# One core, a four-layer transformer stack: the shared expert's chunks put into loops, and the rows of empty routing slots written to DRAM during attention

## The chip, the core and the metric

The kernel runs on one core of a Trainium2 chip. Its engines are TensorE (PE, matrix products; PEld is its weight load), VectorE (DVE), ScalarE (ACT), GpSimd (POOL) and SyncE (SP). Each has its own instruction stream, and they meet through semaphores. SP issues DMAs, and POOL issues the indirect ones, whose rows go to places given by an index. The metric is the time of one launch in microseconds (us) on the device, and less is better.

## What is computed

Eight sublayers on 4 x 1024 tokens of 128 features, each `x = x + f(layernorm(x))`. The change touches the first four: attention with 16 heads of 8 (layers 0 and 1), a gated mixture of experts in which every token goes to its two best of eight experts and to a shared one (layer 0), and a mixture in which every token goes to one of eight experts (layer 1).

```python
# layer 0, feed-forward
topk_logits, topk_idx = jax.lax.top_k(xf @ gate_w.T, 2)
topk_w = jax.nn.softmax(topk_logits)
for e in range(8):
    y = silu(xf @ wg[e].T) * (xf @ wu[e].T) @ w_down[e].T
    out = out + comb[:, e:e + 1] * y          # comb: topk_w, scattered to the experts
shared = silu(xf @ sg_gate.T) * (xf @ sg_up.T) @ sg_down.T
return shared + out
# layer 1, feed-forward: out = W2[e] applied to relu(W1[e] x + b1[e]) + b2[e] of the one expert e
```

## The kernel before

The activations stay in SBUF, transposed: `g.xT` and the normalised `g.xn` are 128 features by 4096 tokens, and a chunk is 512 tokens (`CH`), so there are eight chunks (`NCH`). The program is a row of stages (`Stage`). In a stage each engine has a block of its own, and a stage begins only when all engines are through with the one before, SP's waits among them: when a stage ends, SP clears its semaphores, and the next stage begins behind a barrier.

The stages that matter here, in order:

- `attention_stage` (L431). 32 pairs of heads and batches. In a pair PE makes the scores twice: once for the row maxima, which DVE reduces (L640), two pairs ahead, and once transposed, which ACT exponentiates (L625); PE then weighs the values (L564). POOL fetches the next queries and keys from DRAM (L478) and splits the maxima (L487). SP sends the maxima of the pair after next through DRAM into rows of the queries (`rows`, L511 and L514), which PE waits for before that pair, and stores the results (L523, L525). ACT's code is four pairs written out (m = 0) and a loop over the others, four pairs an iteration.
- `pick_stage` (L999), name f0r. Routing of layer 0: logits, the two best experts, and for each of the 8192 token copies the number of its slot. Slots stand in 39 blocks of 256 (`PICK_BLOCKS`), so that a block has one expert; 9984 slots in all, of which some stay empty. A slot's row is 132 floats (528 bytes): 128 features and a tail of four, with the row's place in the result and its weight. SP first writes all 9984 rows as zeros into `f0_sent` in DRAM (L1036), waits for that, and then writes their tails, each with a place of its own behind the results (L1039), and waits for those too (L1040). So rows of empty slots hold zeros, and a place that disturbs nothing.
- `pick_glu_stage` (L1150), name f0. POOL scatters the 64 tiles of 128 token rows to their slots (L1187), and SP, when all have landed, loads the slots back, six tiles of 128 at a time (L1203, `f_xs`). Meanwhile PE, ACT and DVE compute the shared expert, chunk by chunk: `shared_up` (L1218, L1219), SiLU (L1301), product (L1347), `shared_down` (L1226), addition to `g.xT` (L1340). PE's order is up(0), up(1), down(0), up(2), down(1) and so on, all written out. Then come the 39 blocks (L1235 and on), whose results POOL scatters to `f0_back` (L1193).
- `top1_stage` (L1431), name f1r, and `expert_stage` (L1614): the same for layer 1, with 5888 slots in 23 blocks. POOL clears a buffer `empty` of 46 rows a partition (L1465), DVE puts the places in (L1534), and SP writes it to `f1_sent` in one DMA (L1472) and waits. DVE and PE then look for each expert's threshold in 14 rounds (L1544 to L1560).

Of the kernel before, what the change touches and what calls it, by code (L numbers as in the profile page):

```python
# [14 lines left out]
F32 = mybir.dt.float32  # L15
# [48 lines left out]
class Weights:  # L64
# [16 lines left out]
    def load(self, sp):  # L81
        for tile, source in self.moves:
            sp.dma_start(tile, source, allow_slow_non_contiguous=True).then_inc(self.here, 16)

# [346 lines left out]
def attention_stage(nc, g, name, vsb, qstk, kstk, num, den, scale):  # L431
# [3 lines left out]
    with Stage(nc, name) as s:  # L435
# [24 lines left out]
        UNITS, CUTS = 32, 16  # L460

        with nc.Block() as block:
            @block.gpsimd
            def _(pool):
# [148 lines left out]
            def _(act):  # L613
# [128 lines left out]
def attention(nc, g, name, qkv, out, rope, scale, factor, ahead):  # L742
# [5 lines left out]
    with nc.sbuf_tensor(f"{name}_v", [P, NT, P], F32) as vsb:  # L748
        qkv_stage(nc, g, name + "_qkv", qkv, vsb, qstk, kstk, rope, ahead)
        attention_stage(nc, g, name + "_att", vsb, qstk, kstk, num, den, scale)  # L750
# [235 lines left out]
class Picked:  # L986
# [3 lines left out]
    def __init__(self, nc, ctx):  # L990
# [4 lines left out]
        self.sent = nc.dram_tensor("f0_sent", [PICK_SLOTS, PICK_WIDE], F32, kind="Internal").ap()  # L995
        self.back = nc.dram_tensor("f0_back", [2 * TOK + PICK_SLOTS, P], F32, kind="Internal").ap()


def pick_stage(nc, g, name, w, picked):  # L999
# [4 lines left out]
    n_rows = PICK_SLOTS // P  # L1004
    with Stage(nc, name) as s:
# [5 lines left out]
        zero, tail = s.sb("zero", [P, PICK_WIDE]), s.sb("tail", [P, n_rows, 4])  # L1011
# [9 lines left out]
        zeroed, numbered, own_ready, cleared = (s.sem(x) for x in ("zeroed", "numbered", "own_ready", "cleared"))  # L1021
        by_tile = lambda ps: ps[:, :].rearrange("p (t e) -> p t e", e=e)
        with nc.Block() as block:
            @block.gpsimd
            def _(pool):
                pool.memset(zero[:, :], 0.0).then_inc(zeroed, 1)
                pool.wait_ge(w.here, w.all)
                found.pad(pool)
                pool.memset(tail[:, :, :], 0.0).then_inc(zeroed, 1)
# [31 lines left out]
            def _(dve):  # L1061
# [12 lines left out]
                dve.wait_ge(zeroed, 3)  # L1074
                dve.tensor_scalar(tail[:, :, 0], number[:, :], float(2 * TOK), None, ALU.add).then_inc(numbered, 1)
                link(dve.tensor_copy(rows[:, 0, :, P], number[:, 0:NT]))
                link(dve.tensor_copy(rows[:, 1, :, P], number[:, NT:2 * NT]))
# [72 lines left out]
def pick_glu_stage(nc, g, name, w, picked, ahead):  # L1150
# [6 lines left out]
    with Stage(nc, name) as s:  # L1157
# [24 lines left out]
        with nc.Block() as block:  # L1182
            @block.gpsimd
            def _(pool):
                rows = picked.rows[:, :].rearrange("p (t d) -> p t d", d=PICK_WIDE)
                for t in range(2 * NT):
# [26 lines left out]
            def _(pe):  # L1213
                def shared_up(c):
                    for t in range(2):
                        if c >= 1:
                            pe.wait_ge(s_h, 2 * (c - 1) + t + 1)
                        pe.matmul(za[:, t, :], shared[:, t, :], g.xn[:, cols(c)], start=True, stop=True)  # L1218
                        pe.matmul(zb[:, t, :], shared[:, 2 + t, :], g.xn[:, cols(c)], start=True, stop=True).then_inc(s_ready, 1)  # L1219

                def shared_down(c):
                    if c >= 2:
                        pe.wait_ge(s_added, c - 1)
# [1534 lines left out]
```

## Time and profile before

| | |
|---|---|
| time of the launch, median of 3 | 3518.85 us (3512.96 to 3518.86) |
| the profiled execution's own time | 3530.75 us |
| its span, first to last instruction | 3529.0 us |
| TensorE clock granted, mean | 0.886 of full speed |
| busy: PE, DVE, ACT, POOL | 77%, 71%, 52%, 25% |
| first attention / pick stage / shared expert / blocks of f0, begin at | 213 us (first evacuation) / 881 / 922 / 1025 |

Rows of the timeline give start, duration, engine, line, operation, tiles and, in brackets, how long the engine stood idle before and what it waited for. "PEq" and "SPq" are an engine's sequencer; a wait for "PEq L1023" is the barrier of the block in line 1023. "issue" and "remote" mean that the profile shows nothing on the core that ended the wait.

### The profile page before, as it was taken

How to read it: one execution, taken by the hardware profiler on the slowest of the kernel's cores; microseconds unless marked ns; L12 is line 12 of the kernel's file. 1: busy time of each engine (PE TensorE's matmuls, PEld its weight loads, DVE VectorE, ACT ScalarE, POOL GpSimd, SP SyncE). 2: the span in 40 equal slices, each digit the busy share in tenths (PEclk: the TensorE clock that was granted, in tenths of full speed). 3: DMA queues.
4: the chain of work that ended last, by engine and by line, in shares of the span. 5: the costliest groups of instructions: out<-in, count | busy, mean ns of one | idle time of the engine just before them, and what ended most of it. 6: DMA issues, size and time to landing. Idle time of an engine off the chain costs nothing. (4 is left out here: it accounts for less than half of the span.)

```text
span 3529.0 us, 43620 instructions
## 1 busy us (share of the span) xinstructions
PE 2701.9 (77%) x12690; PEld 967.9 (27%) x12690; DVE 2505.7 (71%) x2942; ACT 1823.1 (52%) x3161; POOL 882.6 (25%) x985
## 2 busy tenths in 40 slices
PE   6499999984469649999998424867777777996666
PEld 3022222221136412222222114622222232332222
DVE  4699999963236469999996271288999975446548
ACT  2188888881224128888888102355555531224233
POOL 3311111100446221111110006416777740000000
PEclk8599999996789759999999657987999998998878
DMA  4200101003522330100100312111000000001010
GB/s 120 91 24 23 28 23 28 23 15 89 90 70 67 106 117 24 28 24 24 27 23 15 102 35 74 48 51 38 6 12 12 7 0 1 0 0 59 6 42 24
DMA packets 161483, 140.96 MB, mean 40 GB/s; under 512 B 51941, under 2 KB 135781, under 8 KB 160984
## 3 DMA queue, kind: packets, MB, share of 16 engines
q1 hardware_dynamic: 142040, 98.68, 10.5%
q0 software_dynamic: 19328, 40.87, 3.8%
q8 instruction: 57, 0.93, 0.1%
q14 instruction: 58, 0.48, 0.0%
HBM read 73.85 MB, written 65.62 MB: 40 GB/s over the span
## 5 line engine op out<-in xcount | busy, mean ns | idle before, releaser
L640 DVE TENSOR_REDUCE a_att_mx<-a_att_s 128x2 f32<-128x1024 f32 x1024 | 1204.9, 1219 | 77.8 <-PE a_att_s L551 65.7
L625 ACT ACTIVATE a_att_pt<-a_att_st 128x512 f32<-128x512 f32 x2048 | 1064.5, 603 | 246.9 <-PE a_att_st L577 246.3
L577 PE MATMUL a_att_st<-a_att_qst,a_att_kst 50*128 50x512 bf16 x2048 | 620.7, 385 | 63.9 <-ACT a_att_pt L625 51.6
L551 PE MATMUL a_att_s<-a_att_kst,a_att_qst 50*128 50x512 bf16 x2048 | 524.8, 399 | 85.1 <-DMA a_att_kst<-a_kstk 52.2
L564 PE MATMUL a_att_av<-a_att_pt,a_att_vst 128*32 128x512 f32 x4096 | 547.2, 607 | 0.0
L577 PEld LDWEIGHTS a_att_st<-a_att_qst,a_att_kst 50*128 50x128 bf16 x2048 | 157.9, 94 | 727.1 <-ACT a_att_pt L625 668.7
L2191 POOL TENSOR_TENSOR g_xn<-m2s_hs,m2s_cb 128x1024 f32<-128x1024 f32 x128 | 300.8, 2355 | 119.0 <-DVE m2s_hs L2158 68.7
L2158 DVE TENSOR_TENSOR_SCAN m2s_hs<-m2s_da,m2s_bps 128x1024 f32<-128x1024 f32 x128 | 292.7, 2287 | 4.4
L487 POOL CAST a_att_mt_in<-a_att_nmax 128x16 bf16<-128x16 f32 x64 | 12.6, 196 | 1072.7 <-DVE a_att_nmax L648 1072.7
L2074 PE MATMUL m2s_yps<-g_xn,g_ident 128*128 128x512 f32 x512 | 242.8, 597 | 0.9
L2130 ACT COPY m2s_cb<-m2s_cps 128x1024 f32<-128x1024 f32 x128 | 129.5, 1012 | 184.1 <-POOL g_xn L2191 182.5
L551 PEld LDWEIGHTS a_att_s<-a_att_kst,a_att_qst 50*128 50x128 bf16 x2048 | 112.8, 94 | 240.1 <-DVE a_att_mx L640 170.6
L2153 DVE TENSOR_TENSOR m2s_bps<-m2s_dtx,m2s_bps 128x1024 f32<-128x1024 f32 x128 | 154.6, 1208 | 3.9 <-POOL m2s_dtx L2177 3.9
L2125 ACT ACTIVATE m2s_da<-m_dt,m2s_aneg 128x1024 f32<-128x1024 f32 x128 | 147.4, 1151 | 0.0
L2094 PE MATMUL m2s_bps<-m_bcs,m2s_sel 96*128 96x512 bf16 x256 | 79.2, 392 | 85.2 <-DVE m2s_hs L2158 82.5
L163 POOL MEMSET n_mean_w<- 128x128 f32 x8 | 1.6, 204 | 565.9 <-POOLq L917 232.6
L959 ACT ACTIVATE f_sg<-f_gp 128x512 f32<-128x512 f32 x72 | 43.0, 597 | 181.5 <-PE f_cp L948 181.5
L971 DVE TENSOR_TENSOR f_h<-f_sg,f_up 128x512 f32<-128x512 f32 x72 | 49.5, 688 | 121.8 <-ACT f_sg L959 121.8
L270 ACT ACT_TABLE_LOAD x9 | 11.5, 1283 | 226.6 <-PEq L696 108.1
L2074 PEld LDWEIGHTS m2s_yps<-g_xn,g_ident 128*128 128x128 f32 x512 | 97.0, 191 | 85.2 <-issue 63.9
L564 PEld LDWEIGHTS a_att_av<-a_att_pt,a_att_vst 128*32 128x32 f32 x4096 | 80.9, 108 | 129.5 <-issue 102.8
L1193 POOL DMA_INDIRECT f_back<-f_yr,f_to x78 | 74.6, 957 | 77.5 <-DVE f_yr L1387 41.8
(477 smaller groups left out, 3681.5 us busy)
## 6 DMA issues: line engine op xcount, KB each, us to landing
a_att_qst<-a_qstk POOLq DMA_DIRECT2D x128, 100.0 KB, 2.5
a_att_kst<-a_kstk POOLq DMA_DIRECT2D x128, 100.0 KB, 2.6
a_qstk<-a_qkv_part SPq DMA_DIRECT2D x96, 128.0 KB, 1.9
a_kstk<-a_qkv_part SPq DMA_DIRECT2D x96, 128.0 KB, 2.0
f_xs<-f_sent SPq DMA_DIRECT2D x20, 396.0 KB, 5.8
f_sent<-f0r_zero SPq DMA_DIRECT2D x1, 5148.0 KB, 22.7
a_num<-a_att_oev SPq DMA_DIRECT2D x256, 16.0 KB
a_out_nm<-a_num SPq DMA_DIRECT2D x16, 256.0 KB, 3.4
```

The source lines that it names most:

```text
L551: mm = pe.matmul(s1[:, cut % 2, h, :], qst[u][64 * h:64 * h + STACK, qt * P:(qt + 1) * P], kst[u][64 * h:64 * h + STACK, kh * CH:(kh + 1) ...
L564: mm = pe.matmul(av[32 * gr:32 * gr + 32, :], vst[u][:, kt, h, :], pt[:, 4 * (kt % 4) + 2 * half + h, :], start=kt == 0, stop=kt == 7)
L577: pe.matmul(st[:, e % 3, :], kst[u][64 * h:64 * h + STACK, kt * P:(kt + 1) * P], qst[u][64 * h:64 * h + STACK, half * CH:(half + 1) * CH], ...
L625: act.activation(pt[:, e % 16, :], st[:, e % 3, :], ACT.Exp, scale=scale).then_inc(exp_done, 1)
L640: dve.tensor_reduce(mx[:, par, 2 * cut:2 * cut + 2], s1[:, cut % 2, :, :], AX.X, ALU.max).then_inc(s1_used, 1)
L2074: mm = pe.matmul(yps[:, f, :], g.ident[:, :], hc[:, k % 4, f * CH:(f + 1) * CH], start=n == 0, stop=n == NS - 1)
L2094: mm = pe.matmul(bps[:, k % 2, f, :], sel[:, n:n + 1].to_broadcast([96, P]), bcs[:, (2 * (q // 2) + f) * CH:(2 * (q // 2) + f + 1) * CH], ...
L2125: act.activation(da[:, k % 4, :], dt[:, q % 2, span(q)], ACT.Exp, scale=aneg[:, q % 2, n:n + 1]).then_inc(da_done, 1)
L2130: act.copy(cb[:, k % 2, :], both(cps[:, :, :])).then_inc(c_copied, 1)
L2153: dve.tensor_tensor(over, dtx[:, q % 2, :], over, ALU.mult).then_inc(dbx_done, 1)
L2158: dve.tensor_tensor_scan(hs[:, k % 3, :], da[:, k % 4, :], over, 0.0, ALU.mult, ALU.add).then_inc(scan_done, 1)
L2191: pool.tensor_tensor(hc[:, k % 4, :], hs[:, k % 3, :], cb[:, k % 2, :], ALU.mult).then_inc(hc_done, 1)
```

## The change

A class `Blank` now owns the writing of the empty rows, one object for each of the two expert layers. Its `make` and `fill` stand in `attention_stage`: POOL clears a tile of 128 x 128 zeros and a tile of tails, counts the places with an iota and puts them in, once, after the fetch for the fifth pair. Its `send` stands on ACT's queue between the fourth pair and the loop: one DMA for the 512 bytes of each row, one for the 16 bytes of each tail, with no wait between them. ACT waits for both at the end of the attention stage, and POOL again ahead of the scatters. What SP wrote and waited for in f0r and f1r is gone, and so are the 5888-row buffer and the DVE operations that made the places. The shared expert is a loop on each engine: PE and DVE take two chunks an iteration (4 iterations), ACT one (8 iterations).

```diff
+    def fill(self, pool):
+        pool.memset(self.zero[:, :], 0.0).then_inc(self.zeroed, 1)
+        pool.memset(self.tail[:, :, :], 0.0).then_inc(self.zeroed, 1)
+        pool.iota(self.serial[:, :], pattern=[[P, self.n]], base=self.first, channel_multiplier=1).then_inc(self.counted, 1)
+        pool.wait_ge(self.zeroed, 2)
+        pool.wait_ge(self.counted, 1)
+        pool.tensor_copy(self.tail[:, :, 0], self.serial[:, :]).then_inc(self.ready, 1)
+
+    def send(self, act):
+        act.wait_ge(self.ready, 1)
+        act.dma_start(self.sent[:, :, 0:P], self.zero[:, :].unsqueeze(1).to_broadcast([P, self.n, P])).then_inc(self.done, 16)
+        act.dma_start(self.sent[:, :, P:P + 4], self.tail[:, :, :]).then_inc(self.done, 16)
...
                 for hp in range(4, PAIRS):
                     split_max(hp - 2)
                     fetch(0, hp, hp - 3)
+                    if hp == 4:
+                        blank.fill(pool)
...
                 for u in range(4):
                     pair(0, u, u > 0)
+                blank.send(act)
                 with act.Fori(1, NPAIR // 4) as m:
                     for u in range(4):
                         pair(m, u, True)
+                act.wait_ge(blank.done, 32)
                 sums(NPAIR // 4 - 1, 3)
...
-            @block.sync
-            def _(sp):
-                sent = picked.sent.rearrange("(i p) d -> p i d", p=P)
-                sp.wait_ge(zeroed, 1)
-                sp.dma_start(sent, zero[:, :].unsqueeze(1).to_broadcast([P, n_rows, PICK_WIDE])).then_inc(cleared, 16)
-                sp.wait_ge(cleared, 16)
-                sp.wait_ge(numbered, 1)
-                sp.dma_start(sent[:, :, P:PICK_WIDE], tail[:, :, :]).then_inc(cleared, 16)
-                sp.wait_ge(cleared, 32)
...
                 rows = picked.rows[:, :].rearrange("p (t d) -> p t d", d=PICK_WIDE)
+                pool.wait_ge(picked.blank.done, 32)
                 for t in range(2 * NT):
...
                 def shared_up(c):
                     for t in range(2):
-                        if c >= 1:
-                            pe.wait_ge(s_h, 2 * (c - 1) + t + 1)
+                        pe.wait_ge(s_h, 2 * c)
...
-                for c in range(NCH + 1):
-                    if c < NCH:
-                        shared_up(c)
-                    if c >= 1:
-                        shared_down(c - 1)
+                with pe.Fori(0, NCH // 2) as m:
+                    for u in range(2):
+                        shared_up(2 * m + u)
+                        shared_down(2 * m + u, u)
...
-                for c in range(NCH):
+                with act.Fori(0, NCH) as c:
                     for t in range(2):
                         act.wait_ge(s_ready, 2 * c + t + 1)
-                        if c >= 1:
-                            act.wait_ge(s_h, 2 * (c - 1) + t + 1)
+                        act.wait_ge(s_h, 2 * c)
                         act.activation(sg1[:, t, :], za[:, t, :], ACT.Silu).then_inc(s_silu, 1)
...
-                pool.memset(empty[:, :, :], 0.0).then_inc(zeroed, 1)
...
-                sp.dma_start(routed.sent.rearrange("(i p) d -> p i d", p=P), empty[:, :, :]).then_inc(cleared, 16)
-                sp.wait_ge(cleared, 16)
```

SP's queue between the norm stage and the blocks of f0, before (f0r's own DMAs in the middle; L50 clears a semaphore, in brackets the semaphores waited for):

```order
L155 UNCONDITIONAL_BRANCH
L50 ISA [waits barrier_Pool_Activation_PE_DVE_SP_release]
L50 ISA x14
L1032 UNCONDITIONAL_BRANCH
L1036 DMA f_sent<-f0r_zero 128x78x132 [waits f0r_zeroed]
L1039 DMA f_sent<-f0r_tail 128x78x4 [waits f0r_numbered,f0r_cleared]
L1023 UNCONDITIONAL_BRANCH [waits f0r_cleared]
```

and at the same place now, up to the first load of the slots:

```order
L182 UNCONDITIONAL_BRANCH
L50 ISA [waits barrier_Pool_Activation_PE_DVE_SP_release]
L50 ISA x14
L50 ISA [waits barrier_Pool_Activation_PE_DVE_SP_release]
L50 ISA x13
L1216 UNCONDITIONAL_BRANCH
L1223 DMA f_xs<-f_sent 128x6x132 [waits f0_scattered]
```

Both DMAs and their waits have left SP's queue, which has no block in f0r any more. ACT's queue in the first attention stage, the fourth pair and the start of the loop, as it is now (`a_att_pt` are the exponentials; before, the two rows L109 and L110 were not there):

```order
L655 ACTIVATE a_att_pt<-a_att_st 128x512 [waits a0_att_st_ready] x32
L648 COPY a_att_oev<-a_att_av 128x512 [waits a0_att_out_done0,a0_att_av_ready]
L655 ACTIVATE a_att_pt<-a_att_st 128x512 [waits a0_att_st_ready] x25
L109 DMA f_sent<-a_att_zero 128x78x128 [waits a0_att_blank_ready]
L110 DMA f_sent<-a_att_tail 128x78x4
L661 UNCONDITIONAL_BRANCH
L661 ISA
```

They stand ahead of all exponentials of the pairs 4 to 31. ACT's whole part in the shared expert was 16 SiLUs behind one table load; now it is this loop body, run eight times:

```order
L1313 UNCONDITIONAL_BRANCH
L1313 ISA
L1317 ACT_TABLE_LOAD [waits f0_s_h]
L1317 ACTIVATE f_sg<-f_za 128x512 [waits f0_s_ready]
L1315 REGISTER_ALU
L1317 ACTIVATE f_sg<-f_za 128x512 [waits f0_s_h,f0_s_ready]
```

The table load has moved into the loop.

## Rows read from the trace of the kernel before

**Rows 1.** The page: span.

```profile
span 3529.0 us, 43620 instructions
```

**Rows 2.** Timeline of DVE, the end of f0r and the start of f0.

```profile
904.73 0.20 DVE L1111 CAST f_slot<-f0r_place 128x64 int32<-128x64 f32 x1
921.71 0.48 DVE L1332 TENSOR_TENSOR f_hit<-f_block_k,f_ends 128x312 f32<-128x312 f32 x1 [16.79 <-PEq L1023]
```

**Rows 3.** Waits of SP from 850 to 1010 us: total, times, longest.

```profile
SPq L1039 <- DMA f_sent<-f0r_zero: 21.4, 1, 21.4
SPq L1023 <- DMA f_sent<-f0r_tail: 16.4, 1, 16.4
```

**Rows 4.** Timeline, from the norm stage into f0r.

```profile
877.69 2.48 DVE L237 TENSOR_TENSOR g_xn<-g_xn,n_row 128x512 f32<-128x512 f32 x4 [2.21 <-PE n_row L204]
880.94 0.21 POOL L1026 MEMSET f0r_zero<- 128x132 f32 x1 [23.59 <-POOLq L155]
```

**Rows 5.** The scatters of f0: ns min/median/max, first and last start.

```profile
L1187 POOL DMA_INDIRECT f_sent<-f_rows,f_slot x64: 954/958/1055, 922.4 to 1002.1; - x64
```

**Rows 6.** Timeline of SP, and landing times in f0.

```profile
1004.40 32.69 SPq L1203 DMA_DIRECT2D f_xs<-f_sent  x6
...
f_xs<-f_sent SPq DMA_DIRECT2D x20, 396.0 KB, 5.8
```

**Rows 7.** Timelines of DVE, ACT and PE during the shared expert.

```profile
932.88 1.29 DVE L1347 TENSOR_TENSOR f_h<-f_sg,f_zb 128x512 f32<-128x512 f32 x2 [3.90 <-PE f_xp L1226]
939.15 1.28 DVE L1347 TENSOR_TENSOR f_h<-f_sg,f_zb 128x512 f32<-128x512 f32 x2 [4.38 <-PE f_xp L1226]
1007.72 1.28 DVE L1347 TENSOR_TENSOR f_h<-f_sg,f_zb 128x512 f32<-128x512 f32 x2 [32.42 <-issue]
...
995.75 0.60 ACT L1301 ACTIVATE f_sg<-f_za 128x512 f32<-128x512 f32 x1 [10.60 <-issue]
...
1008.47 2.08 PE L1218 MATMUL f_za<-g_xn,area 128*128 128x512 f32 x2 [27.28 <-issue]
1016.25 1.13 PE L1218 MATMUL f_za<-g_xn,area 128*128 128x512 f32 x2 [0.85 <-DVE f_h L1347]
...
1025.35 0.66 PE L1235 MATMUL f_xp<-g_ident,f_xs 128*128 128x128 f32 x4 [0.78 <-DVE g_xT L1340]
```

**Rows 8.** Windows: length, busy PE, PEld, DVE, ACT, POOL, clock, DMA, GB/s.

```profile
265.00:285.00 20.00, 19.15 (x134) 4.71 (x132) 19.29 (x19) 17.28 (x34) 2.77 (x7) 1.00 0.10 26
905.00:921.00 16.00, 0.00 (x0) 0.00 (x0) 0.00 (x0) 0.00 (x0) 0.00 (x0) 0.50 1.12 10
```

**Rows 9.** Timelines of ACT, SP and POOL in the first attention, fifth pair.

```profile
272.77 0.58 ACT L618 COPY a_att_oev<-a_att_av 128x512 f32<-128x512 f32 x1
...
275.70 0.37 SPq L511 DMA_DIRECT2D a_att_turned_max<-a_att_mt_out  x1
277.30 1.32 SPq L514 DMA_DIRECT2D a_att_qst<-a_att_turned_max  x2
...
232.73 0.20 POOL L487 CAST a_att_mt_in<-a_att_nmax 128x16 bf16<-128x16 f32 x1 [16.50 <-DVE a_att_nmax L648]
```

**Rows 10.** SP's issues of eight DMAs of 1024 rows: first three, other five.

```profile
L1210 SPq DMA_DIRECT2D f_rows<-f_back x3: 377/579/583, 1156.6 to 1157.6; - x3
...
L1210 SPq DMA_DIRECT2D f_rows<-f_back x5: 1737/1737/2153, 1158.2 to 1166.0; - x5
```

**Rows 11.** DMA issues: KB each, median us from issue to landing.

```profile
f_sent<-f0r_zero SPq DMA_DIRECT2D x1, 5148.0 KB, 22.7
f_sent<-f1r_empty SPq DMA_DIRECT2D x1, 3036.0 KB, 14.0
f_sent<-f0r_tail SPq DMA_DIRECT2D x1, 156.0 KB, 16.8
```

**Rows 12.** Waits of SP from 2020 to 2130 us, in f1r.

```profile
SPq L1460 <- PEq L1460: 66.7, 1, 66.7
```

**Rows 13.** DMA queues from 320 to 720 us: the instruction queues, all rows.

```profile
q14 instruction: 1, 0.01, 0.0%
```

More of the change, by code:

```diff
@@ L83, in load, with __init__, make @@
             sp.dma_start(tile, source, allow_slow_non_contiguous=True).then_inc(self.here, 16)
+class Blank:
+    def __init__(self, nc, g, name, sent, first):
+        self.sent, self.first, self.n = sent.rearrange("(i p) d -> p i d", p=P), first, sent.shape[0] // P
+        self.done = g.ctx.enter_context(nc.semaphore(f"{name}_blank"))
+    def make(self, s):
+        self.zero, self.tail = s.sb("zero", [P, P]), s.sb("tail", [P, self.n, 4])
+        self.serial = s.sb("serial", [P, self.n], mybir.dt.int32)
+        self.zeroed, self.counted, self.ready = s.sem("zeroed"), s.sem("counted"), s.sem("blank_ready")
+    def fill(self, pool):
[9 more added lines that the diff above has]
+        act.dma_start(self.sent[:, :, P:P + 4], self.tail[:, :, :]).then_inc(self.done, 16)
 def chunk(c):
@@ L739, in _, with attention @@
                         pe.matmul(ps[:, u, :], wo[:, :], cx[:, u, :], start=True, stop=True).then_inc(proj_ready, 1)
-def attention(nc, g, name, qkv, out, rope, scale, factor, ahead):
+def attention(nc, g, name, qkv, out, rope, scale, factor, ahead, blank):
     qstk = nc.dram_tensor(f"{name}_qstk", [STACK, HEADS, TOK], BF16, kind="Internal").ap()
@@ L1073, in _ @@
                 link(dve.tensor_tensor(number[:, :], number[:, :], pre_ps[:, 0:1].to_broadcast([P, n_rows]), ALU.add))
-                dve.wait_ge(zeroed, 3)
-                dve.tensor_scalar(tail[:, :, 0], number[:, :], float(2 * TOK), None, ALU.add).then_inc(numbered, 1)
+                dve.wait_ge(zeroed, 1)
                 link(dve.tensor_copy(rows[:, 0, :, P], number[:, 0:NT]))
-                link(dve.tensor_copy(rows[:, 1, :, P], number[:, NT:2 * NT]))
+                dve.tensor_copy(rows[:, 1, :, P], number[:, NT:2 * NT]).then_inc(numbered, 1)
                 link(dve.tensor_tensor_scan(block_k[:, :], g.ones[:, 0:PICK_BLOCKS], g.ones[:, 0:PICK_BLOCKS], -1.0,
@@ L1215, in shared_up, with shared_down @@
                     for t in range(2):
-                        if c >= 1:
-                            pe.wait_ge(s_h, 2 * (c - 1) + t + 1)
[L1218 to L1223, printed above, removed]
+                        pe.wait_ge(s_h, 2 * c)
+                        pe.matmul(za[:, t, :], shared[:, t, :], g.xn[:, chunk(c)], start=True, stop=True)
+                        pe.matmul(zb[:, t, :], shared[:, 2 + t, :], g.xn[:, chunk(c)], start=True, stop=True).then_inc(s_ready, 1)
+                def shared_down(c, u):
+                    pe.wait_ge(s_added, c - u)
                     for t in range(2):
                         pe.wait_ge(s_h, 2 * c + t + 1)
-                        mm = pe.matmul(xp[:, c % 2, :], shared[:, 4 + t, :], h1[:, t, :], start=t == 0, stop=t == 1)
+                        mm = pe.matmul(xp[:, u, :], shared[:, 4 + t, :], h1[:, t, :], start=t == 0, stop=t == 1)
                     mm.then_inc(s_y, 1)
@@ L1336, in _ @@
                 dve.tensor_copy(expert_i[:, :], expert[:, :]).then_inc(known, 1)
-                def shared_add(c):
-                    dve.wait_ge(s_y, c + 1)
-                    dve.tensor_tensor(g.xT[:, cols(c)], g.xT[:, cols(c)], xp[:, c % 2, :], ALU.add).then_inc(s_added, 1)
-                for c in range(NCH):
-                    for t in range(2):
-                        dve.wait_ge(s_silu, 2 * c + t + 1)
-                        if c >= 1:
+                with dve.Fori(0, NCH // 2) as m:
+                    for u in range(2):
+                        c = 2 * m + u
+                        for t in range(2):
+                            dve.wait_ge(s_silu, 2 * c + t + 1)
                             dve.wait_ge(s_y, c)
-                        dve.tensor_tensor(h1[:, t, :], sg1[:, t, :], zb[:, t, :], ALU.mult).then_inc(s_h, 1)
-                    if c >= 1:
-                        shared_add(c - 1)
-                shared_add(NCH - 1)
+                            dve.tensor_tensor(h1[:, t, :], sg1[:, t, :], zb[:, t, :], ALU.mult).then_inc(s_h, 1)
+                        dve.wait_ge(s_y, c + 1)
+                        dve.tensor_tensor(g.xT[:, chunk(c)], g.xT[:, chunk(c)], xp[:, u, :], ALU.add).then_inc(s_added, 1)
+                dve.wait_ge(s_added, NCH)
                 def take_x(i):
@@ L1443, in top1_stage @@
         above = s.sb("above", [P, 3, e, NT])
[L1444 to L1446 removed]
+        serial, number = s.sb("serial", [P, NT]), s.sb("number", [P, NT])
+        place_ps_ready = s.sem("place_ps_ready")
         count_k = s.sb("count_k", [P, BLOCKS])
@@ L1646, in _ @@
                 place = lambda t: bass.IndirectOffsetOnAxis(ap=routed.slot[:, t:t + 1], axis=0)
+                pool.wait_ge(routed.blank.done, 32)
                 for t in range(NT):
```

52 lines of the change are left out of this document (23 added, 29 removed).

## The prediction

> **What bounds the kernel now.** I read the page for the span [rows 1], then, since the stages follow each other behind barriers and have different limits, the timeline and the waits of the stages that the diff touches. No engine's total helps: only what ends last in each of them counts.
>
> *The end of f0r.* The last computation is DVE's cast of the slot numbers, which ends at 904.93 us. The next stage begins at 921.71, and DVE's 16.79 us of idle time are put down to the barrier [rows 2]. SP is who comes late: it waited 21.4 us for the DMA of zeros, could only then send the tails, and waited 16.4 us more for them [rows 3]. Nothing computes from 905 to 921, while the DMA engines are busy throughout, at 10 GB/s [rows 8]. So this stretch is set by SP's two DMAs in a row.
>
> *The first part of f0.* POOL's 64 scatters go from 922.4 to 1002.1 + 0.96 = 1003.1, one every 1.26 us [rows 5]. SP issues the first load of the slots at 1004.40, and such a load lands after 5.8 us [rows 6], so the blocks could start at 1010.2. They start at 1025.35, when the addition of the last chunk of the shared expert is done [rows 7]. So the shared expert ends last here, by 15.1 us, in this execution. That is odd, since a chunk takes 6.27 us while all runs well (932.88 to 939.15), and eight take some 54 with the start. But from about 945 on, what waits for PE's results waits long: ACT 10.60 us once, DVE 32.42 us for what three such steps hide, and PE then 27.28 us for DVE [rows 7]. No row shows what holds these signals; they come on time before 945 and after 1004, when the last scatter is out. I call it the slow stretch.
>
> *Attention.* In 20 us of it PE works 19.15, DVE 19.29 and ACT 17.28 [rows 8]. No engine there has more than 14% to spare, so a stall on ACT's queue is soon one of the stage.
>
> *f1r.* SP waited 66.7 us at the barrier for PE [rows 12], after its own DMA had landed: what it writes there is covered by the search for the thresholds.
>
> **The change part by part.**
>
> *SP's two DMAs and their waits leave f0r.* DVE's 904.93 then ends it. From the last work of a stage to the first of the next the norm stage shows 880.94 - (877.69 + 2.48) = 0.77 us [rows 4], so f0 begins at 905.7, not 921.7. Gain 16.0. Everything up to the first load moves with it, since POOL's scatters, SP's wait for them and the load follow from that start. POOL's new wait ahead of the scatters is for DMAs that ended hundreds of microseconds earlier.
>
> *The loops.* Per chunk the same six products, two SiLUs, two products on DVE and one addition. The order is stricter: up(c + 1) now stands behind down(c). But before, the chunk period was already a round through all three engines (6.27), and I find the same parts in the new one: down's second half, four products, SiLU, product, again 6.1 to 6.5 with the branches. The table load in ACT's loop takes its turn after DVE's product, while PE works on four more matrices. So eight chunks end at about 905.7 + 54 = 960, if nothing holds them, and the slots cannot be there before 1010.2 - 16.0 = 994.2. Cost nothing, with 34 us of cover; without cover it would be some 8 x 0.3 = 2.4. With the slow stretch, which began some 23 us after the first scatter and ended with the last, PE has the same three signals a chunk to give as before, so I expect the same 1025.35 - 1003.1 = 22.3 us from the end of the scatters to the blocks. Gain nothing beyond the 16.0. I take this value because no part of the change touches what I can see of that stretch; the other end, that it vanishes, is the first rival.
>
> *POOL's fill.* Two clears, an iota and a copy. POOL idles 16.5 us before each split of the maxima [rows 9], and the iota, which no row shows, would have to take longer than that to be seen: bounds 0 and, if it took 20 us, 4. I take 0.
>
> *ACT's two issues.* SP takes 0.37 to 0.58 us for an issue with nothing or little in its queue [rows 10]; two are about 0.95 us for ACT. PE is then short of a free bank, and part of it reaches DVE's reductions; ACT's own slack (2.7 in 20 us) takes the rest. I take 0.5 per attention stage, 1.0 in all, bounds 0 and 1.9.
>
> *The transfers beside attention.* The zeros took 22.7 us and the tails 16.8, alone in the queue [rows 11]; in the second attention there are 46/78 of the rows, so I estimate 14.0 and 9.9. They run beside SP's chain for the next pair: in the fifth pair, ACT's evacuation is at 272.77, its eighth step, so the pair began at about 268.3 and the next begins at 287.9. SP issues the maxima at 275.70 and fetches them at 277.30 [rows 9]; with two more microseconds they are there by about 281, which leaves 7. POOL's fetches have more. The core's DMA is busy one tenth of the time [rows 8]. If both queues share the engines packet by packet, the chain of 4 to 5 us becomes one of perhaps 8, within the slack. I take 0; the other end is a rival.
>
> The Trainium skill agrees on the sharing ("DMA: Bandwidth & Descriptors", section on queues, rings and completion order): SP and ACT each own a row of rings on the same 16 engines, and an engine goes round between them packet by packet. By that rule the term is the 0 that I took. No DMA of ACT stands in this trace, so it can't be checked here.
>
> *f1.* Nothing: 66.7 us of cover [rows 12].
>
> Sum: -16.0 + 1.0 = -15.0 against the profiled execution (3530.75, span 3529.0). The median of the three others is 3518.85, 11.9 less, so the execution that I read was slower than those, and I can't say where; if the slow stretch is weaker in them, both kernels wait for the slots and the 16.0 stays. So 3518.85 - 15.0 = **3504**.
>
> **The rivals.**
>
> *The slow stretch goes with the written-out code.* For it: it is in this stage alone that all three engines run written-out code beside scatters for 80 us. Against: before 945 the same code runs well beside the same scatters. Then the blocks start when the slots land, 15.1 earlier, less 1.5 for PE, which has stood idle and runs at half clock first (2.08 against 1.13 us for a pair of products) [rows 7]: 3504 - 13.6 = 3490.
>
> *SP waits behind ACT's DMAs.* This is the one that ends slower. If the chain's DMAs come through only when ACT's are written, then in the first attention the maxima that SP sends at 275.70 wait until 268.3 + 22.7 = 291.0 (behind the zeros) or 307.8 (behind the tails too), and are with PE 4.9 later, where 287.9 is due: 8.0 or 24.8 late. In the second, zeros end 14.0 and tails 23.9 after the start, due is 19.6: 0 or 9.2 late. Together 8 (time 3512) or 34 (3538). It decides for slower once the delays exceed 15 + 7. For it: every DMA of the queues in this trace that could tell was SP's own. Against: POOL's and SP's go side by side in every pair.
>
> *ACT stands in its second issue.* SP's issues of 1024 rows took 0.58 up to the third and 1.74 to 2.15 from the fourth, 3072 rows outstanding [rows 10]. If rows are what fills the queue, the tails must wait until 9984 - 3072 = 6912 rows are gone, 15.7 us at the rate of the zeros, and 2816 rows or 6.7 us in the second attention: ACT stands, and with it the stage, 22 us, 3525. If the number of DMAs is what fills it, two are too few, and nothing is lost. I hold the second likelier, since the zeros themselves, three times as many rows, were issued in no more time.
>
> *The branches cost.* If each turn of ACT's loop had to wait as long as the slow stretch made ACT wait, 10.6 us, eight would take 85, the shared expert would end at 960 + 85 = 1045, and the blocks start 36 us after the 1009.3 that I expect: 3540. Against: 400 us of the attention loop show one packet on the instruction queues [rows 13], so going back does not fetch code there. The Trainium skill says otherwise ("Runtime: NRT & Kernel Launch", instruction fetch mechanics): a taken branch whose target is outside the two pages held forces a fetch. By that rule, and with short bodies here, the loops might just as well cost nothing; the trace's long attention body contradicts it for PE.
>
> **How the numbers follow.** Chances: my forecast 0.60; the slow stretch gone 0.12; SP late by 8 us 0.06, by 34 us 0.06; ACT standing 0.08; branches 0.03; small things of either sign 0.05. The likeliest case has its own range of 3501 to 3508: gain 15.5 to 16.3, ACT 0 to 1.9, and 3 for what SP's chain might lose. The range for all takes in the slow stretch gone and SP late by 8: 3488 to 3513, 0.81 with part of the small things. A measurement of this kernel can tell about 0.2%, 7 us: faster is below 3511.8, slower above 3525.9. Faster: 0.60 + 0.12 + half of 0.06 + 0.03 = 0.78. Same: the other half, most of ACT standing, 0.11. Slower: 0.11.
>
> **What the profile after would show.** DVE's idle time before `f_hit` below 1 us, and f0's first scatter within 1.5 us of the cast of the slots. From the last scatter to the first block 22 us if the slow stretch stays, 7 if it goes. In attention, the DMA issues on ACT of about 0.4 us each, the pair after them within a microsecond of the 19.6 of the others; a pair that is 5 us or more longer would be one of two rivals: ACT's idle time put down to PE and PE's to the maxima's rows, or a long issue on ACT itself. f1r unchanged. I am wrong altogether if f0 does not begin some 16 us earlier after f0r's first instruction.

## The result and the profile after

The changed kernel is slower: 3531.02 us (3521.43 to 3550.68, 18 runs) against 3515.9 us (3499.51 to 3529.97, 18 runs), ratio 1.005 with a 95% interval of 1.0034 to 1.0067. The forecast was 3504. The profiled execution took 3541.91 us.

What was to be removed is gone. The timeline of DVE at the end of f0r, which answers to [rows 2], and the scatters and the first block of f0, which answer to [rows 5, 7], in the changed kernel:

```profile
935.91 0.19 DVE L1130 CAST f_slot<-f0r_place 128x64 int32<-128x64 f32 x1
936.63 0.48 DVE L1348 TENSOR_TENSOR f_hit<-f_block_k,f_ends 128x312 f32<-128x312 f32 x1 [0.53 <-PEq L1055]
...
L1207 POOL DMA_INDIRECT f_sent<-f_rows,f_slot x64: 964/968/1056, 937.4 to 1017.6; - x64
...
1023.45 1.09 PE L1253 MATMUL f_xp<-g_ident,f_xs 128*128 128x128 f32 x4 [36.58 <-DMA f_xs<-f_sent]
```

DVE idles 0.53 us where it idled 16.79. The blocks begin 4.8 us after the last scatter (1018.6), not 22.3, and PE waits 36.58 us for the slots, so the slow stretch is not in this execution.

What was lost is in attention. The timeline of ACT in the kernel before, the third to fifth evacuation (L618) of the first attention:

```profile
233.23 0.58 ACT L618 COPY a_att_oev<-a_att_av 128x512 f32<-128x512 f32 x1
...
253.06 0.58 ACT L618 COPY a_att_oev<-a_att_av 128x512 f32<-128x512 f32 x1
...
272.77 0.58 ACT L618 COPY a_att_oev<-a_att_av 128x512 f32<-128x512 f32 x1
```

The timelines of ACT and SP in the changed kernel, where the evacuation is L648, around the send in the first attention and its issues in the second:

```profile
233.98 0.59 ACT L648 COPY a_att_oev<-a_att_av 128x512 f32<-128x512 f32 x1
...
248.81 0.40 ACTq L109 DMA_DIRECT2D f_sent<-a_att_zero  x1
249.25 18.86 ACTq L110 DMA_DIRECT2D f_sent<-a_att_tail  x1
268.31 3.53 ACT L655 ACTIVATE a_att_pt<-a_att_st 128x512 f32<-128x512 f32 x7 [18.90 <-issue]
273.08 0.59 ACT L648 COPY a_att_oev<-a_att_av 128x512 f32<-128x512 f32 x1 [1.24 <-PE a_att_av L594]
...
276.42 0.37 SPq L541 DMA_DIRECT2D a_att_turned_max<-a_att_mt_out  x1
286.81 1.33 SPq L544 DMA_DIRECT2D a_att_qst<-a_att_turned_max  x2
...
1386.51 0.40 ACTq L109 DMA_DIRECT2D f_sent<-a_att_zero  x1
1386.94 9.67 ACTq L110 DMA_DIRECT2D f_sent<-a_att_tail  x1
```

ACT issues the zeros in 0.40 us and then stands 18.86 us in the issue of the tails. The evacuations L648 are a clock for the pairs: from 233.98 to 273.08 are 39.10 us, and from that one to the next (294.08) 21.00. The same two pairs of before take 19.83 and 19.71, and all others of the changed kernel 19.3 to 19.8, but for the last of each stage. So the send costs 19.3 + 1.3 us here and 10.1 in the second attention (29.91 for 19.85), 30.7 together. SP's fetch of the maxima waits 10.0 us where it waited 1.2 [rows 9]. ACT's stand hides most of that, since it has delayed the next pair too.

The windows of the changed kernel (columns as in [rows 8]) show the DMA engines full during the stand, and a second loss, at the end of both attentions:

```profile
250.00:268.00 18.00, 1.25 (x11) 0.16 (x8) 1.38 (x2) 0.00 (x0) 0.00 (x0) 0.63 1.17 237
...
781.00:806.00 25.00, 20.16 (x131) 4.56 (x130) 3.43 (x5) 22.23 (x44) 0.42 (x2) 1.00 0.03 4
806.00:832.00 26.00, 23.93 (x93) 3.32 (x89) 0.00 (x0) 13.88 (x27) 0.00 (x0) 0.54 0.02 3
1937.00:1958.00 21.00, 19.70 (x74) 2.69 (x74) 0.00 (x0) 10.53 (x21) 0.00 (x0) 0.51 0.00 0
```

When the last maxima are done, PE has about 4 of 5 us to do. In the execution of before it kept its 2.4 GHz there, as a window of its last pair shows:

```profile
791.00:796.00 5.00, 3.99 (x25) 0.97 (x25) 0.00 (x0) 4.35 (x10) 0.00 (x0) 1.00 0.00 0
```

In the changed kernel the granted clock falls to 0.5, 1.2 GHz, PE becomes the bound, and the last evacuation comes 25.81 and 24.65 us after the one before, not 16.71. That is 9.1 + 7.9 us.

So the two profiled executions differ by 30.7 (send) + 17.0 (clock) - 15.7 (f0r) - 22.8 (f0) + some 2 elsewhere = +11. The experiments show which of these belong to the change.

### The profile page after: what moved, and what is told of

It reads as the page before. It is cut to its first block and busy times, and to the rows that moved or that the text cites. A ratio compares the mean times of both kernels' runs of the same rounds, so it can differ in the third digit from the quotient of the medians.

```text
span 3540.2 us, 43746 instructions
## 1 busy us (share of the span) xinstructions
PE 2723.0 (77%) x12690; PEld 968.5 (27%) x12690; DVE 2506.9 (71%) x2940; ACT 1832.7 (52%) x3168; POOL 881.5 (25%) x990
## 5 line engine op out<-in xcount | busy, mean ns | idle before, releaser
L607 PE MATMUL a_att_st<-a_att_qst,a_att_kst 50*128 50x512 bf16 x2048 | 629.9, 391 | 89.4 <-ACT a_att_pt L655 75.3
L594 PE MATMUL a_att_av<-a_att_pt,a_att_vst 128*32 128x512 f32 x4096 | 561.7, 622 | 0.0
L410 PE MATMUL a_qkv_ps<-g_xn,area 128*128 x96 | 56.1, 746 | 47.1 <-DVE a_qkv_t L433 26.0
## 6 DMA issues: line engine op xcount, KB each, us to landing
f_sent<-a_att_zero ACTq DMA_DIRECT2D x1, 4992.0 KB, 25.7
```

The costliest lines, as they stand in the source:

```text
L594: mm = pe.matmul(av[32 * gr:32 * gr + 32, :], vst[u][:, kt, h, :], pt[:, 4 * (kt % 4) + 2 * half + h, :], start=kt == 0, stop=kt == 7)
L607: pe.matmul(st[:, e % 3, :], kst[u][64 * h:64 * h + STACK, kt * P:(kt + 1) * P], qst[u][64 * h:64 * h + STACK, half * CH:(half + 1) * CH], ...
```

## The experiments

All kernels of a group ran on one chip with the kernel before: 3522.65 us (35 runs) beside e1 to e4, 3550.72 (14 runs) beside e5 to e8, 3545.37 (26 runs) beside e9 to e12. The ratios are not the quotients of these medians (for e1 that would be 0.9975). The lengths of stages, in us from the first instruction of one to that of the next, and the time from the last scatter's end to the first block, by the timeline of each profiled execution (the expectations count an attention stage some 1.3 us shorter):

| | attention 0 | f0r | f0 | attention 1 | scatter to block |
|---|---|---|---|---|---|
| before | 682.0 | 40.7 | 259.5 | 681.2 | 22.3 |
| changed | 712.0 | 25.0 | 236.7 | 699.4 | 4.8 |
| e1 loops | 699.4 | 36.6 | 236.7 | 681.2 | 4.7 |
| e2 blank | 701.2 | 24.8 | 236.5 | 691.6 | 4.8 |
| e3 tails in router | 705.4 | 25.2 | 236.1 | 689.3 | 4.7 |
| e4 pieces on SP | 691.5 | 25.0 | 235.6 | 690.6 | 4.7 |
| e5 before again | 691.3 | 39.9 | 271.0 | 682.5 | 28.3 |
| e6 swap | 708.4 | 24.8 | 269.2 | 686.2 | 29.0 |
| e7 apart | 691.4 | 25.0 | 276.1 | 681.6 | 32.4 |
| e8 filler | 682.5 | 24.9 | 267.3 | 683.2 | 27.0 |
| e9 filler, before | 682.1 | 36.7 | 270.8 | 681.3 | 26.5 |
| e10 sends added | 701.1 | 36.2 | 262.3 | 691.5 | 22.5 |
| e11 whole on SP | 697.9 | 25.0 | 267.1 | 682.0 | 26.9 |
| e12 filler again | 682.5 | 25.0 | 267.2 | 683.1 | 27.0 |

**e1_loops: the loops alone.** In the kernel before (PE's part; DVE and ACT likewise):

```diff
-                for c in range(NCH + 1):
-                    if c < NCH:
-                        shared_up(c)
-                    if c >= 1:
-                        shared_down(c - 1)
+                with pe.Fori(0, NCH // 2) as m:
+                    for u in range(2):
+                        shared_up(2 * m + u)
+                        shared_down(2 * m + u, u)
```

> The kernel before with the loops of the shared expert alone; the empty slots are written in f0r as before. Theory A (the slow stretch of f0 is real in every execution and belongs to the written-out code): the first block starts when the first slots land, some 5 us after the last scatter instead of 22.3, and f0 is some 17 to 23 us shorter, as in the profile of the changed kernel: about 3495. Theory B (the slow stretch is a matter of the single profiled execution of before; in the median both kernels wait for the slots): the median stays at 3516 within 7 us, whatever its profile shows. Both expect that attention and f0r stay as in before (681, 680 and 41 us).

Measured: 3513.98 us, ratio 0.9996 (0.9973 to 1.0019). The loops neither cost nor bring what a measurement can tell. The profile has half clock in the last two pairs of its first attention, 17.0 us in all, which is why that stage is 699.4 us.

**e2_blank: all but the loops.** The same lines of the changed kernel the other way round.

> The changed kernel with the shared expert written out again as in before. Both theories expect ACT's second issue to take 18.9 us in the first and 9.7 us in the second attention, and the pairs around it to be 21 and 10 us longer. Theory B: all of the change's cost is this, less the 16 of f0r: +15, about 3531, as the changed kernel itself. Theory A: the loops' 20 us are missing as well: about 3548.

Measured: 3526.68 us, ratio 1.0014 (0.9995 to 1.0033). In the profile the two pairs with the send are 38.35 and 29.80 us, +18.5 and +10.0, as expected, and f0 is as short as with the loops. So theory A falls: written-out code and a fast f0 go together. The ratio is lower than the 1.0043 of theory B, which lies above its interval. This profile shows full clock to the end of both attentions, and the 12 runs spread over 12 us only, where the changed kernel's spread over 29. The mean granted clock of each run says what may differ. On this chip the 35 runs of before fall into two sets: 14 with a mean clock of 0.882 or more took 3501 to 3514 us, 21 with 0.881 or less took 3522 to 3535. All 12 runs of e2 have 0.882 or more, and 7 of the changed kernel's 18 have less. So e2 seems to have met half clock more rarely than either, which lowers its ratio; why it should, no run tells.

**e3_tails_router: one DMA on ACT.** POOL makes the tails in f0r and f1r, and ACT waits for its one DMA at the end of attention.

```diff
-        act.dma_start(self.sent[:, :, P:P + 4], self.tail[:, :, :]).then_inc(self.done, 16)
+    def send_tail(self, sp):          # called on SP at the start of f0r and f1r
+        sp.wait_ge(self.ready, 1)
+        sp.dma_start(self.sent[:, :, P:P + 4], self.tail[:, :, :]).then_inc(self.done, 16)
+        sp.wait_ge(self.done, 32)
```

> The changed kernel, but ACT sends only the zeros in attention; the tails are filled by GpSimd and sent by SP at the start of f0r and f1r. Theory Q (ACT stood because its second DMA found the queue full of the first one's rows): one issue of 0.4 us on ACT, no pair of attention more than 2 us longer, f0r still some 25 us since 16.8 us of tails fit into it: 16 us faster than before, about 3500. Rival (SP's maxima wait behind the zeros): SP's fetch of the maxima comes only after the zeros have landed, 25 us after their issue; the pair after the issue is some 8 us longer in the first attention and 0 in the second: about 3508. Last pair of each attention: 16.7 us if TensorE keeps its full clock, 25 if not; which of the two I can't tell beforehand.

Measured: 3508.04 us, ratio 0.9974 (0.995 to 0.9997). Its interval just leaves out 1, but 3 of its 12 runs have a mean clock of 0.881 or less where 21 of 35 of before have, so part of this may be the clock; that it is faster at the same clock is not shown by the times. ACT's issue takes 0.40 us and ACT does not stand. But SP's maxima do come late beside the zeros. The timelines of SP and ACT, and the wait of PE:

```profile
255.80 0.37 SPq L551 DMA_DIRECT2D a_att_turned_max<-a_att_mt_out  x1
262.98 1.87 SPq L554 DMA_DIRECT2D a_att_qst<-a_att_turned_max  x2
...
272.48 1.57 ACT L665 ACTIVATE a_att_pt<-a_att_st 128x512 f32<-128x512 f32 x3 [3.88 <-PE a_att_st L617]
...
PE a_att_st L617 <- DMA a_att_qst<-a_att_turned_max: 3.7, 1, 3.7
```

From the maxima's issue to their fetch are 7.2 us, not 1.6 [rows 9]. The fetch at 262.98 is 10 us before the zeros have landed (issued at 247.90, landed 25.1 us later), so the maxima are slowed beside the zeros, but not held until their end, which is what the rival expected. Two pairs are longer by 0.3 and 5.5 us, 5.8 in all, in the first attention, and none in the second. Half clock comes on top in this profile (28.14, 24.98 and 24.65 us at the ends).

**e4_pieces_sp: small pieces on SP.** In `result`'s place on SP, behind each pair:

```diff
+    def send(self, sp, at, n):
+        sp.dma_start(self.sent[:, bass.ds(at, n), 0:P], self.zero[:, :].unsqueeze(1).to_broadcast([P, n, P])).then_inc(self.done, 16)
+        sp.dma_start(self.sent[:, bass.ds(at, n), P:P + 4], self.tail[:, bass.ds(at, n), :]).then_inc(self.done, 16)
...
+                        blank.send(sp, blank.each * (PAIRS * b + hp), blank.each)
```

> The changed kernel, but both DMAs are cut into small ones (384 rows of zeros and 384 of tails in f0, 128 and 128 in f1's loop, 384 and 384 behind it), and SP sends one pair of them after each pair's result; nothing is issued on ACT. Theory Q: no issue takes more than 1 us, every pair of attention stays at 19.6 to 19.8 us, f0r at 25: about 3500. Rival (the DMA work as such slows attention, however it is issued): the pairs with pieces are longer, together some 20 us: about 3520 or more.

Measured: 3511.61 us, ratio 0.9977 (0.995 to 1.0003). The groups of these DMAs (ns min/median/max of an issue, and landing times of the zeros):

```profile
L111 SPq DMA_DIRECT2D f_sent<-a_att_zero x58: 361/404/451, 204.6 to 1927.9; - x58
L112 SPq DMA_DIRECT2D f_sent<-a_att_tail x58: 371/405/1056, 205.3 to 1928.4; - x58
DMA to landing us min/median/max: 1.6/2.2/2.5
```

No pair is longer than 19.82 us, until the last, which ran at half clock in both attentions (25.78 and 24.61). So the same bytes cost nothing when they go in small pieces on a queue on which nobody computes. Small pieces on ACT were not tried. What keeps this kernel from 3500 in its profile is the clock.

**e5_before_again: the kernel before, profiled again.**

> The kernel before, unchanged, profiled a second time, since the slow stretch of f0 was in its first profile and in none of the four experiments, written-out code or not. Theory B (it belonged to that one execution): f0 takes some 237 us instead of 259.5, the shared expert ends 50 us after its start, and the blocks begin about 5 us after the last scatter. Theory A (it belongs to this kernel's own arrangement of zeros, tails and written-out code): 259 us again, the first block 22 us after the last scatter. The last pair of each attention takes 16.7 or 25 us.

Measured: 3549.07 us. The slow stretch is there again, 28.3 us from the last scatter to the first block. With e6 to e12, all at 22.5 to 32.4 us, and the changed kernel with e1 to e4, all at 4.7 or 4.8, it goes with the group of runs, not with the code: loops and written-out code are on both sides. Neither theory had put it so. The unprofiled runs seem to have it too: the fastest run of the kernel before took 3501 us beside e1 to e4, and 3538 and 3534 beside e5 to e8 and e9 to e12, 33 to 37 us more, where f0 is 26 to 40 us longer. On which chip the first profile of before was taken isn't known. One of two attentions ended at half clock (25.77 us).

**e6_swap: tails first.** The two `dma_start` of `send` changed places.

> The changed kernel with ACT's two DMAs in the other order, tails first. Theory Q (what fills the queue is rows, whatever their size; in the changed kernel the second issue ended when some 1,800 to 2,400 rows of the first were left): the tails' issue takes 0.4 us, the zeros' issue stands until all but that many rows of the tails are gone, about 13 us in the first attention and 6 in the second by the 16.8 and 10 us that they take. Rival S (the 16-byte rows are slow to issue): the tails' issue takes 18.9 and 9.7 us although it is first, and the zeros' 0.4. Rival bytes (megabytes outstanding fill the queue): neither stands, since 0.16 MB are outstanding.

Measured, in the timeline of ACT:

```profile
249.70 0.40 ACTq L109 DMA_DIRECT2D f_sent<-a_att_tail  x1
250.13 11.56 ACTq L110 DMA_DIRECT2D f_sent<-a_att_zero  x1
...
1415.38 0.40 ACTq L109 DMA_DIRECT2D f_sent<-a_att_tail  x1
1415.81 3.62 ACTq L110 DMA_DIRECT2D f_sent<-a_att_zero  x1
```

The second issue stands, whichever it is, and though only 0.16 MB lie ahead of it. It stands less, since tails are through sooner than zeros: they land 18.2 and 10.9 us after their issue. So neither bytes nor slow small rows explain it. Nor does the number of DMAs, since e4 issues two of 384 rows each behind one another in 0.4 us an issue. What is left is the number of rows. Expected were 13 and 6 us. How many rows the queue takes stays open: at an even rate, an estimate from the landing times, 2,500 and 1,900 rows of zeros are left when the stand ends in the changed kernel, and 3,400 and 3,700 of tails here.

The time is 3559.90 us, one run. Though ACT stands 7.3 us less than in the changed kernel, the first attention still loses 12.0 + 6.0 us, against 20.6: SP's maxima wait 6.3 us beside the zeros, and PE now waits 4.2 us for them. The second loses 4.0 + 0.6 us, against 10.1.

**e7_apart: two pairs between the two.** `blank.send` (zeros) after ACT's second pair, `blank.send_tail` after its fourth. They come out 47.1 us apart in the first attention and 39.2 in the second.

> The changed kernel with the zeros sent after the second pair of ACT and the tails after the fourth, 39 us apart; the fill stands ahead of the fetch of the fifth pair. Theory Q: the zeros have landed (25.7 us) when the tails are issued, so both issues take 0.4 us; what is left is SP's maxima behind ACT's rows, 5 us for each of the two in the first attention and none in the second: the first attention about 691 us with full clock, the second 680. Rival S: the tails' issue takes 18.9 and 9.7 us as before.

Measured, timeline of ACT:

```profile
210.71 0.40 ACTq L109 DMA_DIRECT2D f_sent<-a_att_zero  x1
257.80 0.37 ACTq L112 DMA_DIRECT2D f_sent<-a_att_tail  x1
```

Neither stands, in the second attention either. Left are 7.9 and 0.8 us in the first attention, where SP's maxima wait for the rows (up to 9.9 us), and nothing in the second. Both attentions end at full clock. Time 3543.33 us, one run.

**e8_filler: e4 and idle products.** So I call products of PE whose results nobody reads. Where `first` is false, that is in the last two pairs:

```diff
                         def cut(half):
                             if first:
                                 first_cut(n + 2, (u + 2) % 4, m + 1 + (u >= 2), 2 * kt + half)
+                            elif kt >= 1 and half == 0:
+                                if u == 2 and kt == 1:
+                                    pe.wait_ge(s1_used, CUTS * NPAIR)
+                                for h in range(2):
+                                    pe.matmul(s1[:, kt % 2, h, :], qst[u][64 * h:64 * h + STACK, kt * P:(kt + 1) * P],
+                                              kst[u][64 * h:64 * h + STACK, 0:CH], start=True, stop=True)
```

> The kernel of small pieces on SP, and in the last two pairs of each attention seven more pairs of products a pair on TensorE, into PSUM banks that nobody reads any more, so that TensorE is as busy there as in the pairs before. Theory C (the 8 to 9 us at the end of an attention stage are TensorE at half clock, which comes in some executions because its work thins out when the last maxima are done): the granted clock is 1.0 to the end of both stages, the last two pairs take 19.3 to 19.8 and 16.7 to 18 us, and the median falls from 3511.6 to about 3500, with less spread. Rival (the clock falls for another reason): half clock and 24 to 26 us again.

Measured: 3530.71 us (3527.41 to 3536.16) where before takes 3550.72 (3537.72 to 3571.06), ratio 0.9935 (0.9913 to 0.9958). This is the fastest kernel of the study against its own kernel before. The window of its last pair in the first attention, beside that of e4:

```profile
784.00:804.00 20.00, 17.18 (x119) 4.04 (x115) 0.00 (x0) 16.29 (x32) 0.00 (x0) 1.00 0.02 5
```

```profile
787.00:812.00 25.00, 22.93 (x87) 3.12 (x86) 0.00 (x0) 13.25 (x26) 0.00 (x0) 0.52 0.02 4
```

The clock is 1.0 to the end, and the last pairs take 19.41 and 16.71 us: as long as those of before, so the idle products themselves cost nothing.

**e9_filler_before: the idle products alone.** The lines of e8 in the kernel before.

> The kernel before, with only the idle products of the last two pairs of each attention added. Theory C (half clock at the end of a stage of attention is a matter of chance in each execution, one stage in two so far, 8 to 9 us a stage and once 17): full clock to the end of both stages and a median some 8 us below the kernel before, with less spread than its 33 us. Rival (the gain of the last experiment was all in f0r): the same time as before within 2 us.

Measured: 3538.91 us (3533.92 to 3543.57), ratio 0.9977 (0.996 to 0.9994): 8 us by the ratio, and a spread of 10 us instead of 25. The clocks of all runs agree: of the 33 runs of e8, e9 and e12 none has a mean granted clock below 0.883, and 17 of the 40 of the kernel before beside them have 0.881 or less.

**e10_sends_added: the sends without the removal.** The kernel before, with `Blank` in both attentions and nothing taken out.

> The kernel before, with f0r and f1r and the shared expert as they are, and the filling and sending of zeros and tails added to both attentions (into two DRAM tensors of the same shapes that nobody reads). Theory Q prices this at 20 us in the first and 10 in the second attention: 30 us or 0.85% slower than before. If the changed kernel lost its time elsewhere (the loops, the new waits of GpSimd, the branches), this one is less than 0.85% slower by that amount.

Measured: 3570.05 us, ratio 1.0071 (1.0046 to 1.0096), so 25 us with 16 to 34 in the interval. The pairs with the send are 18.3 + 0.3 and 9.8 us longer, and the second issue stands 17.95 and 9.44:

```profile
250.28 0.40 ACTq L109 DMA_DIRECT2D x_sent<-a_att_zero  x1
250.71 17.95 ACTq L110 DMA_DIRECT2D x_sent<-a_att_tail  x1
268.87 3.54 ACT L655 ACTIVATE a_att_pt<-a_att_st 128x512 f32<-128x512 f32 x7 [18.00 <-issue]
```

**e11_sp_whole: both whole DMAs on SP.** `blank.send(sp)` behind `result(0, 3)`; nothing on ACT.

> The changed kernel with both whole DMAs sent by SP, behind its DMAs for the result of the fourth pair; ACT issues nothing. Theory Q: now SP stands 18.9 us in the tails' issue in the first attention and 9.7 in the second, its next maxima are sent behind all the rows, about 38 us after the zeros' issue, 8 to 10 us late in the first attention and 0 to 3 in the second. So attention loses about 9 and 1 instead of 20 and 10, since no computing engine stands. Rival (the rows themselves slow attention): 20 and 10 us again.

Measured: 3542.86 us, one run. SP's timeline and PE's wait in the first attention:

```profile
262.65 0.45 SPq L109 DMA_DIRECT2D f_sent<-a_att_zero  x1
263.15 20.68 SPq L110 DMA_DIRECT2D f_sent<-a_att_tail  x1
283.88 14.23 SPq L541 DMA_DIRECT2D a_att_turned_max<-a_att_mt_out  x1
300.56 1.29 SPq L544 DMA_DIRECT2D a_att_qst<-a_att_turned_max  x2
...
PE a_att_st L613 <- DMA a_att_qst<-a_att_turned_max: 14.0, 1, 14.0
```

SP stands 20.68 us in the tails and then 14.23 more in the issue of the maxima, which I had not counted: they find the queue full of tails. One pair is 15.2 us longer (34.92 for 19.73), and none in the second attention. Expected were 9 and 1.

**e12_filler_again: e8 beside e9.**

> The kernel of small pieces on SP with the idle products, again, beside the kernel before with the same idle products on one chip: both keep full clock in attention, so their difference is what the change itself is worth once its issues cost nothing. By f0r, 11.6 to 15.7 us shorter in the profiles, it is 12 to 16 us, 0.35 to 0.45%. If the loops of the shared expert cost something (nothing showed yet) it is less; if they bring something, more.

Measured: 3529.13 us (3524.56 to 3536.55), ratio 0.996 (0.9941 to 0.9978). Against e9 on the same chip the medians differ by 9.8 us and the two profiled spans by 13.1 (3536.0 and 3522.9), 11.7 of it in f0r. These 10 us are what the change is worth when its DMAs cost nothing, somewhat less than the 12 to 16 expected.

## Why the prediction was wrong

The step that failed is the one on ACT's second issue: "If the number of DMAs is what fills it, two are too few, and nothing is lost. I hold the second likelier, since the zeros themselves, three times as many rows, were issued in no more time." The reason given does not bear on it. The zeros met an empty queue, and so did the tails in e6; what stands is the issue behind them. The rival that I gave 0.08, rows fill the queue, is what happened: it forecast a stand of 15.7 + 6.7 us, and 18.9 + 9.7 were measured. Its 3525 is near the 3531 measured, but in part by luck: as a change it is +6 us, and +15 was measured, since the send cost more than its 22 us and f0r gave less than its 16. [Rows 10] had shown it in the kernel before, on a small scale: three issues of 0.4 to 0.6 us and five of 1.7 to 2.2.

Point by point:

- *The end of f0r, -16.0.* Right in mechanism: f0 begins 0.5 us after the cast of the slots has ended. In the two profiles f0r is 15.7 us shorter. But [rows 3] came from an execution in which both DMAs were slow: in e1, e9 and e10 f0r with its DMAs takes 36.2 to 36.7 us, so the term is rather 11 to 12 there, and 15 by e5 (39.9).
- *ACT's two issues, +1.0.* Wrong, 30.7 in the profile, 25 (16 to 34) by e10. Taken with the term above, -12 or -16 and +31 make +15 to +19, and 15.1 was measured between the medians.
- *SP's maxima beside ACT's rows, 0.* Wrong too, though hidden in the changed kernel. Beside the zeros alone the first attention loses 5.8 us (e3) and 8.7 with the tails sent later (e7), where that rival said 8.0 and the slack of 7 us was to cover a chain grown to 8 us; the second attention loses nothing, as the rival said. That the rival's number is near is luck in part: its mechanism, held until ACT's rows are written, does not fit the zeros, beside which the maxima came 10 us (e3) before the zeros had landed. It fits the tails in the changed kernel, which landed at 249.25 + 37.9 = 287.2, 0.3 us after SP's fetch at 286.81. The Trainium skill, which I had cited here ("DMA: Bandwidth & Descriptors", section on queues, rings and completion order), has the engines go round between the rows of rings packet by packet. By these runs that is no promise of a short wait: with large DMAs in ACT's queue SP waited 5.0 us (second attention of e2) to 10.0 us (first attention of the changed kernel) for its 8 KB, where it waited 1.2.
- *The loops, 0.* Right: 0.9996 in e1.
- *The slow stretch.* I expected it in both kernels, and gave 0.12 to its going with the written-out code. The profile of the changed kernel seemed to prove that rival; e2 and e5 to e12 show that it did not. It comes and goes with the group of runs. Where it is gone the blocks begin 4.8 us after the last scatter, not the 7 that I gave, since the first load lands 3.5 us after its issue (1019.93 to 1023.45) and not after the median of 5.8 us.
- *Branches, POOL's fill, f1r.* Nothing was lost there. The fill takes 0.2 to 0.4 us an operation, and f1r is 92.4 us for 92.7.
- *Where the fifth pair stands.* I read it one pair too late, and so does the table ahead of the change, with its first evacuation at 213 us: the first is at 194.00, the fourth, in the fifth pair, at 253.06. So that pair begins at about 248.6 and not at 268.3, as the changed kernel's issue at 248.81 has it. Since one pair is like the next, no term changes.
- *What I had not seen at all* is the half clock at the end of attention. In the 11 profiles without idle products it came in 9 of 22 attentions, at 7.9 to 9.1 us each and twice 17; in the 3 with them in none of 6. It came with loops and with written-out code, before the change and after it, so I don't count it to the change; that it comes equally often in each is not shown (see e2). It makes much of the spread in which a change of 15 us has to be seen (3501 to 3514 and 3522 to 3535 us by the mean clock, see e2), and a single pair of profiles tells it as loss or gain.

Open: why f0 takes 236 us in one group of runs and 262 to 276 in others; why e2 seems to meet half clock so rarely; and what in the issuing queue holds the second DMA, its room for rows or the writing of the first one's rows, which no run separates.

## What to carry to other kernels

A DMA is not free for the engine that issues it because its transfer is off the critical path: count the rows already in that engine's queue. If they run to thousands, the next issue stands until most are gone, and everything behind it on that engine with it; put such transfers in small pieces on a queue where nobody computes, at least the length of one transfer away from the next, and clear of the small DMAs that someone waits for.

Before a difference of profiles is read as the effect of a change, compare stage by stage with a second profile of the kernel before. Here three of the four large differences did not give the change's size: the slow stretch and the half clock were not its doing, and f0r was only in part.

## What the runs showed of the hardware

- ACT's and SP's queues take an issue in 0.4 us while few rows are in them (384 in e4); with 9984 rows of 512 bytes ahead the next issue stands 18.0 to 20.7 us, with 5888 rows 9.4 to 10.4. In the changed kernel the stand ends 6.4 us before the first DMA has landed (249.25 + 18.86 = 268.1 for 248.81 + 25.7 = 274.5). 16-byte rows fill the queue as 512-byte rows do (e6), but are through sooner, and so the stand is 11.6 and 3.6 us.
- Beside large DMAs of ACT's queue a DMA of 8 KB on SP's, waited for 1.2 us otherwise, was waited for 5.0 to 10.0 us.
- TensorE's clock fell from 2.4 to 1.2 GHz at the end of 9 attentions of 22, while it was still busy 4 of 5 us, and held in the other 13 with the same work. With the idle products it held in 6 of 6.
- The same code took 236 us in f0 in one group of runs (e4) and 267 in others (e8, e12), with no row of the profile that shows what holds the signals.
